# Token mixer of a vision tower: the kqv product contracted over 576 rows, with the last channel's weight row taken from all others and the last 64 rows worked in pairs

## The chip, the core and the metric

The kernel is one program on one core of a Trainium2 chip. The metric is the device time of one execution in microseconds (us), as the median of several runs. The engines are named as in the profile: PE is TensorE (matmuls and transposes), PEld its weight loads, DVE VectorE, ACT ScalarE, POOL GpSimd, SP SyncE, which issues transfers.

## The reference

The whole is a vision tower: a tokenizer with two "performer" blocks, two attentions, a mixture of experts, a state space layer and a gated mixture of experts. The change lies in the tokenizer's second performer block, here called the token mixer. What it computes, cut from the reference:

```python
def _ln(x, g, b):
    mu = jnp.mean(x, -1, keepdims=True)
    var = jnp.var(x, -1, keepdims=True)
    return (x - mu) * jax.lax.rsqrt(var + 1e-05) * g + b

def _performer(x, n1g, n1b, kqvw, kqvb, projw, projb, n2g, n2b, w1, b1, w2, b2, wrand):
    h = _ln(x, n1g, n1b)
    kqv = h @ kqvw + kqvb
    k, q, v = (kqv[..., :EMB], kqv[..., EMB:2 * EMB], kqv[..., 2 * EMB:])
    kp, qp = (_prm_exp(k, wrand), _prm_exp(q, wrand))
    ...
    y = v + (y @ projw + projb)
    h2 = _ln(y, n2g, n2b)
    return y + (jax.nn.gelu(h2 @ w1 + b1, approximate=False) @ w2 + b2)
```

In the token mixer x has 32 images of 256 tokens, each token 576 channels (9 taps of 64). `kqvw` is 576 x 192, all in fp32. A row of x less its mean sums to zero over the 576 channels.

## The kernel before, in words

`tokens` is the token mixer. It works in 16 steps of two images: 512 tokens as four tiles of 128 tokens. `X` holds the patches as they come, `hN` the normalised ones, `hT` the transposed ones, `W` the weights (256 columns: 192 of kqv and 64 of features made from them), `KQ` the product in PSUM, one tile in half a bank, tiles 0 and 1 in one bank and 2 and 3 in the next.

The contraction has 577 rows: 576 channels and a row of ones for the bias. `KT` cuts it into four chunks of 128 rows and one of 65. For each chunk k, `turn(i, k)` makes four transposes into a bank of PSUM, `keep(i, k)` copies the bank to `hT` on ScalarE, and `matmuls(i, j)` makes the five matmuls of tile j.

Each engine has its own program, written out in an order by hand and tied by semaphores. One loop over t lets several pairs of images be in flight. PE's step t is:

```
proj_matmuls(t-6), matmuls(t-1,0), keys_values(t-2), turn_queries(t-2), proj_turn(t-5), matmuls(t-1,1),
turn(t,0), turn(t,1), project_keys(t-2), turn_y(t-3), matmuls(t-1,2), turn(t,3), numerators(t-2),
mlp1(t-3), matmuls(t-1,3), mlp2(t-3), turn(t,4), turn(t,2)
```

The parts at t-5 and t-6 project finished tokens (`PX`, `PXT`, `PO`) and exist from steps 5 and 6 on. The waits that matter: `matmuls(i, 0)` waits for `z` of the pair before, since `KQ` has one buffer, and for all five `hT` chunks. `z` comes from `exponent` on DVE, behind `squares` and `values` on ACT, behind the last matmul of the pair (`kq`). `proj_turn(i)` waits for `po`, the copy of the projection's result by `proj_out` (L1128) on DVE, which stands in DVE's order behind `exponent` (L1067, L1071) and `normalise` (L1061). `normalise` waits for `rstd1` from `root` on POOL (L1008, L1010), which stands on POOL behind `bias_y` (L1028), which waits for `finish` on DVE (L1117), which waits for `mlp2` (L1342). SP issues per step 12 transfers for X (once `normalise` freed the buffer), 4 of results, 6 for `PX` and 1 of `PO`.

`Later` holds what the mixer needs ready: the stage ahead, `patches`, runs its parts beside its own work. `clear` (POOL, at that stage's step 4) zeroes tiles; `load` (SP) fetches weights once seven clears are done; `tensor` and `vector` fold gains and biases into `W` in three hops at the stage's end.

## Time and profile before

| what | value |
|---|---|
| median of 3 runs | 1924.81 us (1924.61 to 1925.4) |
| the profiled execution | 1919.23 us, its span 1917.5 us |
| PE busy in the span | 1602.2 us (84%) |
| DVE, ACT, POOL busy | 1080.6, 816.2, 736.7 us |
| kqv matmuls of the token mixer (L1279) | 640 records, 150.9 us |

The profile is of one execution, so a sum is made against its own 1919.23 us. One fp32 matmul is two records on PE and one transpose is one. PE's matmuls overlap at their ends, so what one costs is read from the start of one group to the start of the next and not from its busy time.

### The profile page before, as it was taken

Reading aid. Unit: us, or ns where it says so; the run is one execution under the profiler, and the core shown is the slowest. Engines: PE = TensorE matmul, PEld = TensorE weight load, DVE = VectorE, ACT = ScalarE, POOL = GpSimd, SP = SyncE. Lnnn points to the kernel's source line nnn. Section 1 sums busy time; section 2 is a strip of 40 time slices with the busy share of each in tenths; the row PEclk is TensorE's granted clock in tenths of the full one; section 3 lists DMA queues with packets and bytes.
Section 4 is the critical chain, followed back from the end, with each engine's and each line's share of the span. In section 5 each row is a group of like instructions: output and inputs, shape, how many; then the busy total and the mean of one; then the engine's idle time right before and its main releaser. Section 6 shows DMA issues by size and latency. Waiting matters only on the chain. (4 is left out here: it accounts for less than half of the span.)

```text
span 1917.5 us, 35003 instructions
## 1 busy us (share of the span) xinstructions
PE 1602.2 (84%) x11224; PEld 1231.6 (64%) x11225; DVE 1080.6 (56%) x3241; ACT 816.2 (43%) x1641; POOL 736.7 (38%) x680
## 2 busy tenths in 40 slices
PE   3889999968999976897988789996499477767997
PEld 2667777747888863775677779995377233347554
DVE  2678888856776633297267523331800599952332
ACT  0457777733555522283145533332355332324221
POOL 2557676721222204252423114442200399930232
PEclk9989999988999977897979669998599799967999
DMA  3243434323334222000000444442500666625321
GB/s 62 45 95 73 83 73 82 75 67 92 105 110 118 68 59 70 1 2 13 1 2 2 131 143 179 167 177 73 129 1 0 178 161 162 156 64 159 101 95 43
DMA packets 219149, 163.90 MB, mean 85 GB/s; under 512 B 115754, under 2 KB 198695, under 8 KB 218525
## 3 DMA queue, kind: packets, MB, share of 16 engines
q1 hardware_dynamic: 206135, 146.94, 28.8%
q0 software_dynamic: 6528, 14.19, 2.6%
q10 hardware_dynamic: 6374, 1.33, 0.4%
q8 instruction: 64, 1.05, 0.2%
q14 instruction: 48, 0.39, 0.1%
HBM read 106.05 MB, written 32.35 MB: 72 GB/s over the span
## 5 line engine op out<-in xcount | busy, mean ns | idle before, releaser
L2156 POOL TENSOR_TENSOR ssm_scan_prod<-ssm_scan_S,ssm_crep 128x1056 f32<-128x1056 f32 x48 | 159.4, 3320 | 146.8 <-DVE ssm_scan_S L2173 146.8
L1279 PE MATMUL a_psum<-a2w_W,a_hT 128*128 128x256 f32 (+1 forms) x640 | 150.9, 383 | 5.4 <-DVE a_z L1071 4.5
L755 PE MATMUL a_psum<-a_W,a_hT 126*128 126x256 f32 x512 | 135.3, 397 | 0.0
L1279 PEld LDWEIGHTS a_psum<-a2w_W,a_hT 128*128 128x128 f32 (+1 forms) x640 | 119.9, 192 | 21.2 <-issue 6.6
L2197 PE MATMUL ssm_scan_psum<-ssm_ST,ssm_EW 112*128 112x512 f32 (+1 forms) x288 | 106.0, 506 | 24.0 <-PEq L1908 20.4
L2173 DVE TENSOR_TENSOR_SCAN ssm_scan_S<-ssm_scan_X,ssm_scan_psum 128x1056 f32<-128x1056 f32 x48 | 113.0, 2354 | 5.5 <-ACT ssm_scan_psum L2185 1.2
L2813 ACT ACTIVATE moe_tiles_GT<-moe_tiles_psum,moe_tiles_mine 128x128 f32<-128x128 f32 x240 | 66.4, 376 | 110.6 <-PE moe_tiles_psum L2764 110.5
L2197 PEld LDWEIGHTS ssm_scan_psum<-ssm_ST,ssm_EW 112*128 112x128 f32 x288 | 52.3, 195 | 92.7 <-issue 69.7
L755 PEld LDWEIGHTS a_psum<-a_W,a_hT 126*128 126x128 f32 x512 | 91.1, 193 | 30.9 <-issue 21.9
L543 POOL TENSOR_TENSOR a_rstd<-a_rstd,a_mhalf 128x8 f32<-128x8 f32 x64 | 105.1, 1642 | 5.0
L2185 ACT ACTIVATE ssm_scan_psum<-ssm_scan_psum 128x1056 f32<-128x1056 f32 x48 | 49.7, 1035 | 121.3 <-PE ssm_scan_psum L2197 121.3
L2744 PE MATMUL moe_tiles_psum<-moe_W,moe_tiles_GT 128*128 x480 | 84.5, 326 | 0.0
L2865 DVE TENSOR_TENSOR moe_tiles_Y<-moe_tiles_psum,moe_B 128x192 f32<-128x192 f32 x40 | 14.3, 358 | 124.2 <-PE moe_tiles_psum L2744 124.2
L2053 PE MATMUL ssm_mlp_psum<-ssm_mlp_xT,ssm_mlp_W 96*128 96x260 f32 (+3 forms) x352 | 81.7, 392 | 2.6 <-SPq L1959 2.6
L1028 POOL TENSOR_TENSOR a_yb<-a_y,a2w_b 128x256 f32<-128x256 f32 x16 | 11.6, 725 | 177.1 <-DVE a_O L1117 165.3
L2709 POOL DMA_INDIRECT ys<-moe_tiles_Y,moe_target x40 | 39.4, 986 | 103.9 <-DVE moe_tiles_Y L2865 101.0
L563 POOL TENSOR_TENSOR a_yb<-a_y,a_b 128x512 f32<-128x512 f32 x32 | 40.8, 1277 | 96.9 <-DVE a_O L638 96.9
L2053 PEld LDWEIGHTS ssm_mlp_psum<-ssm_mlp_xT,ssm_mlp_W 96*128 96x128 f32 (+3 forms) x352 | 66.9, 190 | 16.4 <-issue 3.0
L2744 PEld LDWEIGHTS moe_tiles_psum<-moe_W,moe_tiles_GT 128*128 128x128 f32 x480 | 77.2, 190 | 0.0
L2699 POOL DMA_INDIRECT moe_tiles_X<-xs,moe_source x40 | 39.0, 975 | 81.3 <-POOLq L2307 69.4
L2210 PE MATMUL ssm_scan_psum<-ssm_scan_prod,ssm_SEL 128*32 128x264 f32 x384 | 32.8, 415 | 43.5 <-POOL ssm_scan_prod L2156 43.5
L2166 DVE TENSOR_TENSOR ssm_scan_X<-ssm_scan_grep,ssm_brep 128x1056 f32<-128x1056 f32 x48 | 59.2, 1233 | 17.0 <-DMA ssm_scan_grep<-gains 17.0
(654 smaller groups left out, 4059.0 us busy)
## 6 DMA issues: line engine op xcount, KB each, us to landing
ssm_scan_grep<-gains SPq DMA_DIRECT2D x48, 528.0 KB, 4.7
moe_tiles_mine<-moe_W SPq DMA_DIRECT2D x40, 579.0 KB, 3.1
a2w_X<-t SPq DMA_DIRECT2D x192, 96.0 KB
t<-a_O SPq DMA_DIRECT2D x128, 64.0 KB
xrows<-in_x SPq DMA_DIRECT2D x30, 192.0 KB
glu_tiles_mine<-glu_W1r SPq DMA_DIRECT2D x24, 234.5 KB, 3.2
a_X<-xrows SPq DMA_DIRECT2D x60, 91.9 KB, 3.0
a_PX<-t SPq DMA_DIRECT2D x96, 48.0 KB
```

Source lines behind the costliest of these rows:

```text
L543: nc.gpsimd.tensor_tensor(out[:], out[:], mhalf[:], ALU.pow).then_inc(s[done], 1)
L563: nc.gpsimd.tensor_tensor(yb[:], y[:], spread(b2[:], 1, tiles), ALU.add).then_inc(s["yb"], 1)
L755: last = nc.tensor.matmul(KQ[q][:, j, :], hT[0:MAIN, q, PARTS * j:PARTS * j + PARTS], W[0:MAIN, :], start=False, stop=True)
L1279: last = nc.tensor.matmul(KQ[:, j, :], hT[i % 2][0:rows, k, PARTS * j:PARTS * j + PARTS], W[0:rows, k, :], start=(k == 0), stop=(k == 4))
L2053: last = nc.tensor.matmul(ps[0:rows_, (n % 4) * BANK:(n % 4) * BANK + GROUP], W1[0:k, kb, c0:c0 + rows_], xT[0:k, kb, GROUP * g:GROUP * g ...
L2156: nc.gpsimd.tensor_tensor(prod[n % 2][:], S[n % 2][:], crep[:, cols], ALU.mult).then_inc(s_prod, 1)
L2166: nc.vector.tensor_tensor(X[n % 2][:], grep[n % NEWEST][:], brep[:, cols], ALU.mult).then_inc(s_x, 1)
L2173: nc.vector.tensor_tensor_scan(S[n % 2][:], X[n % 2][:], E[n % 2], 0.0, ALU.add, ALU.mult).then_inc(s_scan, 1)
L2185: nc.scalar.activation(E[n % 2], E[n % 2], ACT.Exp).then_inc(s_coef, 1)
L2197: last = nc.tensor.matmul(E[n % 2][:, a:b], EW[:, j, :], ST[:, j // (NCH // 2), HCOLS * h + a:HCOLS * h + b], start=True, stop=True)
L2744: last = nc.tensor.matmul(made(p), GT[p][0:w_, f, :], W2[0:w_, f, bass.ds(e, 1), :].rearrange("p a c -> p (a c)"), start=(f == 0), stop=(f ...
L2813: last = nc.scalar.activation(GT[1 - p][:, f, :], hidT(1 - p, f), ACT.Gelu, bias=mine[(n - 1) % RING][:, BIAS + f:BIAS + f + 1])
```

## The change

The contraction loses its 577th row. After the three hops of weight preparation a fourth makes two small matmuls with constant matrices (`lessall`, `lastmix`, made on POOL in `clear`): their sums take the weight row of channel 575 from every row of `W`. Since normalised channels sum to zero before gains, the product is the same, and row 575 is free: it takes the bias row, and in the data the last of the 64 remaining channels takes the ones. The last 64 rows of `W` then stand twice, in partitions 0 to 63 and 64 to 127.

`normalise` writes 512 channels to `hN` and 63 to a new tile `hR`, whose four slots hold tiles 0, 2, 1, 3, so that two tiles' 64 remaining channels lie side by side. Chunk 4 is two transposes of 128 columns (tiles 0 and 2, tiles 1 and 3) instead of four, its copy has 256 columns instead of 512, and its four matmuls have 64 rows each: tiles 0 and 1 from partitions 0 to 63, tiles 2 and 3 from 64 to 127. All four stand now ahead of the main ones in `matmuls(i, 0)`.

The diff, cut to its core:

```diff
         self.g2, self.n2b, self.b1r = (st.sbuf(n, [PARTS, 1]) for n in ("g2", "n2b", "b1r"))
+        self.lessall, self.lastmix = st.sbuf("lessall", [EMB + 1, PARTS]), st.sbuf("lastmix", [EMB + 1, 2, EMB])
         self.s_clear, self.s_w, self.s_raw, self.s_brow, self.s_gain, self.s_turn, self.s_wt, self.s_feat = (
...
         nc.gpsimd.memset(self.epst[:], EPS).then_inc(self.s_clear, 1)
+        nc.gpsimd.memset(self.lessall[:], 0.0).then_inc(self.s_clear, 1)
+        nc.gpsimd.memset(self.lastmix[:], 0.0).then_inc(self.s_clear, 1)
+        pool.wait_ge(self.s_clear, 9)
+        nc.gpsimd.affine_select(out=self.lessall[:], in_=self.lessall[:], compare_op=ALU.not_equal, fill=-1.0, base=1 - EMB,
+                                pattern=[[0, PARTS]], channel_multiplier=1).then_inc(self.s_clear, 1)
+        nc.gpsimd.affine_select(out=self.lastmix[:], in_=self.lastmix[:], compare_op=ALU.not_equal, fill=1.0, base=0,
+                                pattern=[[0, 2], [-1, EMB]], channel_multiplier=1).then_inc(self.s_clear, 1)
+        pool.wait_ge(self.s_clear, 11)
+        nc.gpsimd.affine_select(out=self.lastmix[:], in_=self.lastmix[:], compare_op=ALU.not_equal, fill=-1.0, base=1 - EMB,
+                                pattern=[[0, 2], [0, EMB]], channel_multiplier=1).then_inc(self.s_clear, 1)
+        pool.wait_ge(self.s_clear, 12)
+        nc.gpsimd.memset(self.lastmix[:, :, EMB - 1:EMB], 0.0).then_inc(self.s_clear, 1)
+        pool.wait_ge(self.s_clear, 13)
+        nc.gpsimd.affine_select(out=self.lastmix[:, :, EMB - 1:EMB], in_=self.lastmix[:, :, EMB - 1:EMB], compare_op=ALU.not_equal, fill=1.0,
+                                base=-EMB, pattern=[[0, 2], [0, 1]], channel_multiplier=1).then_inc(self.s_clear, 1)
...
             last.then_inc(self.s_turn, 1)
-        else:
+        elif hop == 2:
             pe.wait_ge(self.s_wt, 1)
             last.then_inc(self.s_feat, 1)
+        else:
+            pe.wait_ge(self.s_clear, 14)
+            pe.wait_ge(self.s_wt, 2)
+            nc.tensor.matmul(ps[:, two:two + 256], self.lessall[:], self.W[0:EMB + 1, 4, :], start=True, stop=True)
+            nc.tensor.matmul(ps[:, two + 256:two + 512], self.lastmix[:].rearrange("p a b -> p (a b)"), self.W[0:EMB + 1, 4, :], start=True, stop=True).then_inc(self.s_feat, 1)
...
             nc.vector.tensor_copy(self.WT[:, 4, 0:65], ps[:, two:two + 65]).then_inc(self.s_wt, 1)
-        else:
+        elif hop == 2:
             dve.wait_ge(self.s_feat, 1)
             nc.vector.tensor_copy(self.W[:, 0:4, 3 * EMB:], ps[:, three:three + 8 * FEATS].rearrange("p (k f) -> p k f", k=4))
-            nc.vector.tensor_copy(self.W[0:65, 4, 3 * EMB:], ps[0:65, three + 8 * FEATS:three + 10 * FEATS])
+            nc.vector.tensor_copy(self.W[0:65, 4, 3 * EMB:], ps[0:65, three + 8 * FEATS:three + 10 * FEATS]).then_inc(self.s_wt, 1)
+        else:
+            dve.wait_ge(self.s_feat, 2)
+            nc.vector.tensor_tensor(self.W[:, 0:4, :], self.W[:, 0:4, :], spread(ps[:, two:two + 256], 1, 4), ALU.add)
+            nc.vector.tensor_copy(self.W[:, 4, :], ps[:, two + 256:two + 512])
...
                     exponent(t - 2, 0)
-                if isinstance(t, int) and steps + 2 <= t < steps + 5:
+                if isinstance(t, int) and steps + 2 <= t < steps + 6:
                     later.vector(dve, ps, t - steps - 2)
...
                     sum_keys(t - 2)
-                if isinstance(t, int) and steps + 1 <= t < steps + 4:
+                if isinstance(t, int) and steps + 1 <= t < steps + 5:
                     if t == steps + 1:
...
     tiles, steps, width = 4, IMAGES // 2, 577
-    dim, COLS = 576, 256
+    dim, main, COLS = 576, 512, 256
     KT = later.KT
...
-        hN, hT = pair("hN", [PARTS, tiles, width]), pair("hT", [PARTS, 5, BANK])
+        hN, hR, hT = pair("hN", [PARTS, tiles, main]), pair("hR", [PARTS, tiles, EMB]), pair("hT", [PARTS, 5, BANK])
         stats = st.sbuf("stats", [PARTS, tiles, 2, 6])
...
             for p in range(2):
-                nc.gpsimd.memset(hN[p][:, :, dim:width], 1.0).then_inc(s["ones"], 1)
+                nc.gpsimd.memset(hR[p][:, :, EMB - 1:EMB], 1.0).then_inc(s["ones"], 1)
             nc.gpsimd.memset(v1[:, :, EMB:EMB + 1], 1.0).then_inc(s["ones"], 1)
...
                 for j in range(tiles):
-                    last = nc.vector.tensor_scalar(hN[i % 2][:, j, 0:dim], X[i % 2][:, j, :], mv[i % 2][:, j, 0:1], rstd[i % 2][:, j:j + 1],
-                                                   ALU.subtract, ALU.mult)
+                    nc.vector.tensor_scalar(hN[i % 2][:, j, :], X[i % 2][:, j, 0:main], mv[i % 2][:, j, 0:1], rstd[i % 2][:, j:j + 1],
+                                            ALU.subtract, ALU.mult)
+                for j in range(tiles):
+                    last = nc.vector.tensor_scalar(hR[i % 2][:, 2 * (j % 2) + j // 2, 0:EMB - 1], X[i % 2][:, j, main:dim - 1], mv[i % 2][:, j, 0:1],
+                                                   rstd[i % 2][:, j:j + 1], ALU.subtract, ALU.mult)
                 last.then_inc(s["norm"], 1)
...
                 wait(act, s["kq"], i - 1)
-                rows = KT[k][1]
-                nc.scalar.copy(hT[i % 2][0:rows, k, :], ps[0:rows, TB[k] * BANK:(TB[k] + 1) * BANK]).then_inc(s[f"th{k}"], 1)
+                n = BANK if k < 4 else half
+                nc.scalar.copy(hT[i % 2][:, k, 0:n], ps[:, TB[k] * BANK:TB[k] * BANK + n]).then_inc(s[f"th{k}"], 1)
...
                         pe.wait_ge(s["ones"], 5)
-                c0, rows = KT[k]
-                for j in range(tiles):
-                    last = nc.tensor.transpose(ps[0:rows, TB[k] * BANK + PARTS * j:TB[k] * BANK + PARTS * j + PARTS], hN[i % 2][:, j, c0:c0 + rows], ident[:])
+                for j in range(tiles if k < 4 else tiles // 2):
+                    frm = hN[i % 2][:, j, PARTS * k:PARTS * k + PARTS] if k < 4 else hR[i % 2][:, 2 * j:2 * j + 2, :].rearrange("p t c -> p (t c)")
+                    last = nc.tensor.transpose(ps[:, TB[k] * BANK + PARTS * j:TB[k] * BANK + PARTS * j + PARTS], frm, ident[:])
                 last.then_inc(s[f"t{k}"], 1)
...
                     wait(pe, s["z"], i)
-                for k, (_, rows) in enumerate(KT):
-                    last = nc.tensor.matmul(KQ[:, j, :], hT[i % 2][0:rows, k, PARTS * j:PARTS * j + PARTS], W[0:rows, k, :], start=(k == 0), stop=(k == 4))
+                    for h in range(2):
+                        for u in range(2):
+                            p0 = EMB * u
+                            nc.tensor.matmul(KQ[:, h + 2 * u, :], hT[i % 2][p0:p0 + EMB, 4, PARTS * h:PARTS * h + PARTS], W[p0:p0 + EMB, 4, :],
+                                             start=(h == 0), stop=False, skip_group_check=True)
+                for k in range(4):
+                    last = nc.tensor.matmul(KQ[:, j, :], hT[i % 2][:, k, PARTS * j:PARTS * j + PARTS], W[:, k, :], start=False, stop=(k == 3), skip_group_check=True)
                 if j == 3:
```

On PE, at the end of a full step of the mixer and the head of the next (`a_hN` and `a_hR` are normalised data, `a_hT` their transposes, `a2w_W` the weights). Before:

```order
L1279 MATMUL a_psum<-a2w_W,a_hT 128x256 x5
L1342 MATMUL a_psum<-a2w_w,a_G 128x128 [waits a2_gelu]
L1342 MATMUL a_psum<-a2w_w,a_G 128x128
L1270 MATMUL a_psum<-a2w_ident,a_hN 65x128 [waits a2_th1]
L1270 MATMUL a_psum<-a2w_ident,a_hN 65x128 x3
L1270 MATMUL a_psum<-a2w_ident,a_hN 128x128 [waits a2_gelu]
L1270 MATMUL a_psum<-a2w_ident,a_hN 128x128 x3
L1279 MATMUL a_psum<-a2w_W,a_hT 128x256 [waits a2_th3,a2_th4,a2_th2,a2_z,a2_th1,a2_th0]
L1279 MATMUL a_psum<-a2w_W,a_hT 128x256 x4
L1291 MATMUL a_psum<-a_kpq,a_v 65x32 [waits a2_exp,a2_ymul]
```

And with the change:

```order
L1312 MATMUL a_psum<-a2w_W,a_hT 128x256 x4
L1375 MATMUL a_psum<-a2w_w,a_G 128x128 [waits a2_gelu]
L1375 MATMUL a_psum<-a2w_w,a_G 128x128
L1298 MATMUL a_psum<-a2w_ident,a_hR 128x128 [waits a2_th1]
L1298 MATMUL a_psum<-a2w_ident,a_hR 128x128
L1298 MATMUL a_psum<-a2w_ident,a_hN 128x128 [waits a2_gelu]
L1298 MATMUL a_psum<-a2w_ident,a_hN 128x128 x3
L1309 MATMUL a_psum<-a2w_W,a_hT 128x256 [waits a2_th3,a2_th4,a2_th2,a2_z,a2_th1,a2_th0]
L1309 MATMUL a_psum<-a2w_W,a_hT 128x256 x3
L1312 MATMUL a_psum<-a2w_W,a_hT 128x256 x4
L1324 MATMUL a_psum<-a_kpq,a_v 65x32 [waits a2_exp,a2_ymul]
```

Two transposes are gone between `mlp2` and the next block; the first block has eight matmuls and the others four, where each had five.

On DVE, from `normalise` to `normalise_y` in a late step. Before:

```order
L1061 TENSOR_SCALAR a_hN<-a2w_X,a_mv,a_rstd 128x576 [waits a2_t2,a2_rstd1]
L1061 TENSOR_SCALAR a_hN<-a2w_X,a_mv,a_rstd 128x576 x3
L1128 COPY a_PO<-a_psum 128x192 [waits a2_h1,a2_pm]
L1110 TENSOR_SCALAR a_yn<-a_y,a_mv,a_rstd 128x64 [waits a2_yt,a2_rstd2]
L1110 TENSOR_SCALAR a_yn<-a_y,a_mv,a_rstd 128x64 x3
```

And with the change:

```order
L1086 TENSOR_SCALAR a_hN<-a2w_X,a_mv,a_rstd 128x512 [waits a2_t2,a2_rstd1]
L1086 TENSOR_SCALAR a_hN<-a2w_X,a_mv,a_rstd 128x512 x3
L1089 TENSOR_SCALAR a_hR<-a2w_X,a_mv,a_rstd 128x63 x4
L1156 COPY a_PO<-a_psum 128x192 [waits a2_h1,a2_pm]
L1138 TENSOR_SCALAR a_yn<-a_y,a_mv,a_rstd 128x64 [waits a2_yt,a2_rstd2]
L1138 TENSOR_SCALAR a_yn<-a_y,a_mv,a_rstd 128x64 x3
```

Four instructions more stand ahead of the copy to `PO`; nothing else on DVE moves there.

## Rows read from the trace of the kernel before

**Rows 1.** Stretches: us, busy us (records) by engine, then PEclk, DMA share, GB/s

```profile
428.90:441.45 12.55, 4.61 (x20) 3.88 (x21) 9.40 (x30) 2.93 (x5) 2.66 (x9) 0.50 0.28 67
591.66:607.31 15.65, 15.49 (x97) 14.02 (x97) 11.07 (x38) 8.23 (x16) 3.95 (x7) 1.00 0.45 130
```

**Rows 2.** PE in order of time: start, us, line, operation, shapes, count, idle before

```profile
498.00 2.40 PE L1279 MATMUL a_psum<-a2w_W,a_hT 128*128 128x256 f32 x10 [0.91 <-DVE a_z L1071]
...
588.71 0.61 PE L1342 MATMUL a_psum<-a2w_w,a_G 128*128 128x128 f32 x4
594.73 0.73 PE L1356 MATMUL a_psum<-a2w_ident,a_PX 128*128 128x128 f32 x5 [0.15 <-issue]
595.30 2.33 PE L1279 MATMUL a_psum<-a2w_W,a_hT 128*128 128x256 f32 x10
597.46 1.04 PE L1270 MATMUL a_psum<-a2w_ident,a_hN 128*128 128x128 f32 x8
598.34 0.33 PE L1307 MATMUL a_psum<-a2w_projw,a_kvT 65*128 65x65 f32 x2
...
604.37 0.61 PE L1342 MATMUL a_psum<-a2w_w,a_G 128*128 128x128 f32 x4
```

**Rows 3.** DVE in order of time, the mixer's start and one late step

```profile
433.90 2.05 DVE L1061 TENSOR_SCALAR a_hN<-a2w_X,a_mv,a_rstd 128x576 f32<-128x576 f32 x4 [1.41 <-POOL a_rstd L1010]
...
589.36 0.42 DVE L1117 TENSOR_TENSOR a_O<-a_psum,a_yb 128x256 f32<-128x256 f32 x1 [0.56 <-PE a_psum L1342]
...
591.94 2.42 DVE L1061 TENSOR_SCALAR a_hN<-a2w_X,a_mv,a_rstd 128x576 f32<-128x576 f32 x4 [0.98 <-POOL a_rstd L1010]
594.28 0.34 DVE L1128 COPY a_PO<-a_psum 128x192 f32<-128x192 f32 x1
594.55 0.97 DVE L1110 TENSOR_SCALAR a_yn<-a_y,a_mv,a_rstd 128x64 f32<-128x64 f32 x4
595.44 2.96 DVE L1046 BATCH_NORM_STATS2 a_stats<-a2w_X 128x6 f32<-128x288 f32 x8
```

**Rows 4.** POOL in order of time, the same late step

```profile
589.93 0.73 POOL L1028 TENSOR_TENSOR a_yb<-a_y,a2w_b 128x256 f32<-128x256 f32 x1 [11.54 <-DVE a_O L1117]
...
590.89 1.02 POOL L1010 TENSOR_TENSOR a_rstd<-a_rstd,a2w_mhalf 128x4 f32<-128x4 f32 x1
```

**Rows 5.** Who waited for whom in the mixer: total us, times, longest

```profile
PE a_psum L1279 <- DVE a_z L1071: 4.5, 4, 1.4
...
PE a_psum L1356 <- issue: 1.4, 9, 0.2
```

**Rows 6.** PE in order of time: narrow matmuls in two other stages

```profile
211.32 0.71 PE L749 MATMUL a_psum<-a_Wrem,a_RQ 32*128 32x256 f32 x8
211.97 1.13 PE L755 MATMUL a_psum<-a_W,a_hT 126*128 126x256 f32 x4
...
1300.93 0.94 PE L2761 MATMUL moe_tiles_psum<-moe_tiles_XT,moe_tiles_mine 64*128 64x128 f32 x12
1301.80 1.38 PE L2764 MATMUL moe_tiles_psum<-moe_tiles_XT,moe_tiles_mine 128*128 128x128 f32 x10
```

**Rows 7.** POOL and DVE in order of time, the stage ahead of the mixer

```profile
90.58 0.19 POOL L541 TENSOR_TENSOR a_rstd<-a_mv,a_eps 128x8 f32<-128x8 f32 x1
...
104.03 1.80 DVE L580 BATCH_NORM_STATS2 a_stats<-a_X 128x6 f32<-128x147 f32 x8 [9.62 <-DMA a_X<-xrows]
```

**Rows 8.** All engines in order of time, the end of that stage

```profile
422.52 2.02 PE L830 MATMUL a_psum<-a_w,a_G 128*128 128x128 f32 x8
...
424.58 0.69 DVE L638 TENSOR_TENSOR a_O<-a_psum,a_yb 128x512 f32<-128x512 f32 x1 [1.26 <-PE a_psum L830]
425.37 1.73 SPq L498 DMA_DIRECT2D t<-a_O  x4
...
428.95 2.97 DVE L1046 BATCH_NORM_STATS2 a_stats<-a2w_X 128x6 f32<-128x288 f32 x8 [3.67 <-PEq L202]
```

**Rows 9.** SP's queue in order of time, the same late step

```profile
594.39 7.62 SPq L99 DMA_DIRECT2D a2w_X<-t  x12
```

## The prediction, made before the change was run

> **What bounds the kernel now.** I read the stretches of the span first, then the token mixer's own stretch engine by engine in order of time, then who waits for whom there. All that the change touches lies in the token mixer, from 428.9 us on [rows 8], plus eight small instructions and one more hop of weight preparation in the stage ahead of it. In a full step of the mixer TensorE works 15.49 us of 15.65, at the full granted clock (1.00, 2.4 GHz), against 11.07 us of VectorE, 8.23 of ScalarE and 3.95 of GpSimd [rows 1]. TensorE is the bound, so what it is spared counts, as long as nothing else is late by then. Two things are nearly late. In four early steps TensorE waits for `z`, 4.5 us together [rows 5]: there a closed loop of TensorE, ScalarE and VectorE sets the step. In ten later steps there is a hole of 0.15 us ahead of line 1356 [rows 2], nine of them visible [rows 5]. That hole is the trace of a second loop: `mlp2` ends, VectorE's line 1117, GpSimd's 1028 and 1010, VectorE's 1061 and 1128, and only then may TensorE turn `PX` (its wait on `po`) [rows 3, 4]. Row by row: `mlp2` starts at 588.71 and line 1128 ends at about 594.6; line 1356 starts at 594.73 [rows 2, 3].
>
> **The change part by part: TensorE.** Five matmuls of 256 columns take from 595.30 to 597.46, 0.433 us each [rows 2]. The fifth of each tile, over 65 rows, costs as much as one over 128, so the four of them are 1.73 us a step. In their place stand four of 64 rows in two pairs. The nearest rows are the twelve records of line 2761, which are the same pattern (64 rows, halves of the array in turn, two banks): 1300.93 to 1301.80, 0.87 us for 12 records of 128 columns, and the eight records of line 749 (32 rows, 256 columns): 211.32 to 211.97, 0.65 us where one after the other they would need 1.73 [rows 6]. Line 749 is two passes of 0.213 us and 0.22 us over, which I read as the weights' load standing bare at the way in and at the way out; line 2761 fits this (six passes of 0.107 and 0.22). So four passes: 4 x 0.213 + 0.22 = 1.07 us. The gain is 0.66 us a step. Its bounds: 0.87 us (nothing bare) and 1.73 + 0.2 (pairs one after the other). In the steps that wait for `z` the load was bare already (2.40 against 2.33 us for the block [rows 2]), so there it is 0.73.
> Eight transposes take 597.46 to 598.34, 0.109 us each [rows 2]; two fewer a step are 0.22 us. They stand between `mlp2` and the next block, in the wait for `z`, so in the four steps that wait they bring nothing.
> All four narrow matmuls move into the first block of the step: that block grows from 2.16 to 2.80 us and the three others shrink by 0.43 each.
>
> **VectorE.** Normalising was four instructions of 576 elements, 591.94 to 594.28 = 2.34 us; undisturbed it is 2.05 [rows 3], so some 0.36 us of it is the last one being held while GpSimd's adds run. Now it is four of 512 and four of 63. Line 1110 is four of 64 elements: 594.55 to 595.44, 0.22 us each; four of 576 take 0.49 apart from the hold. Per element that is (0.49 - 0.22)/512 = 0.53 ns, so a 512 takes 0.46. Sum: 4 x 0.46 + 4 x 0.22 = 2.72 against 1.96, so the edit costs x = 0.76 us. Bounds: 0.3 (the small ones nearly hidden behind their neighbours) to 1.3 (their own 0.3 each and a second hold). I take 0.76, since line 1110 is the same operation on the same engine. The Trainium skill, "VectorE: DVE Perf Modes", section on the TRN2 errata, gives a VectorE instruction from SBUF to SBUF a fixed 58 cycles beside its elements; by that figure the four more would add about 0.24 us, an estimate, and the second loop would not bind. The rows of line 1110 speak against it; it is the second rival below.
>
> **The second loop after the change.** From line 1356 to `mlp2` it runs 594.73 to 604.37 = 9.64 us, all TensorE, with three blocks in it: 9.64 - 1.30 = 8.34. From `mlp2` to line 1356 it runs 588.71 to 594.73 = 6.02, all in the chain over VectorE and GpSimd: 6.02 + 0.76 = 6.78. Together 15.12 us, against 15.66 now (588.71 to 604.37 [rows 2]). TensorE's own work would be 15.49 - 0.66 - 0.22 = 14.6. So this loop binds, TensorE waits 0.4 to 0.5 us a step ahead of the `PX` transposes, and the step gains 0.54 instead of about 1.0. The cost that VectorE takes on is thus not hidden in these steps.
>
> **What has cover.** ScalarE's copy of chunk 4 has 256 columns instead of 512 and is not late now. SyncE issues 23 transfers a step at 0.635 us (twelve take 7.62 [rows 9]), 14.6 us, under 15.12; X has a whole step of slack. GpSimd's eight more instructions (about 1.9 us, from neighbours of 0.1 to 0.3 us and four waits) push `root` of the sixth image from 90.58 on, and TensorE's transposes behind it by 1.3 us, but VectorE stands still until an X transfer lands at 104.03 [rows 7], and SyncE waits only for the first seven clears, which stay where they were. The new hop: TensorE's last matmuls end near 424.5 [rows 8], at the half clock that the mixer's first stretch still has (0.50 [rows 1]); two matmuls of 256 columns there are 1.71 us, then on VectorE 1024 elements, twice line 638's 0.69 less its fixed part, 1.22, and a copy of 0.42, done near 428.1. What ends the block is the last stores, whose issue runs to 427.1 and whose data must land before the mixer starts at 428.9 [rows 8]. Covered by about 0.6 us; if that cover went, it costs that much and no more than 1.
>
> **The sum.** Start: first normalising +0.76, two transposes fewer at half clock (0.50 [rows 1]) -0.43: +0.33. Step 1 -0.66. Steps 2 to 4 -0.73 each, -2.2. Step 5 (`z` wait at its head, no `po` wait) -0.73 - 0.22 = -0.95. Steps 6 to 15: 10 x -0.54 = -5.4. Step 16 has no transposes and no normalising beside it: -0.66. Sum -9.5 us. The tail of dependent short work keeps its length. The profiled execution took 1919.23 us (span 1917.5), so it would be 1909.7; the median of the runs shown is 1924.81, 5.6 us above it, and I take the difference off that: 1915.3 us.
>
> **The rivals.**
> *Pairs don't overlap.* A block of four then costs 1.73 + 0.2 us. TensorE's work falls by nothing (-0.22 + 0.2) and it is the bound again: steps 6 to 15 gain only the 0.15 hole, the others lose 0.1 to 0.2: -0.4 us, 1924.4. The change would not do what it says. Lines 749 and 2761 speak against it, and both write different banks in turn, as the new ones do. The Trainium skill, "TensorEngine Tiling (Array Packing)", section on PSUM pressure, says that row tiles cannot use one PSUM bank at the same time; tiles 0 and 2, or 1 and 3, are in different banks here, so by that rule too they overlap. Chance 0.08.
> *The small instructions are cheap* (x at or under 0.3). Then TensorE's work is the bound, 14.6 us a step: -1.0 x 10 in place of -5.4, -14.1 us, 1910.7. Chance 0.10.
> *The hold spreads (slower).* VectorE's last line-1061 instruction now costs 0.36 us more when GpSimd works beside it. If four more of the eight were held so, x = 0.76 + 1.44 = 2.2, and ten steps change by -1.30 + 2.2 = +0.9: with the -4.1 of the other steps +4.9, 1929.7. It turns slower than before from x = 1.71. Against it: GpSimd runs only line 1023 (0.68 us) and short four-element work in that stretch, and one hold is all that it makes now. The Trainium skill, "SBUF - State Buffer", section on SBUF's two sides, calls the pair of ports that the two engines share an exclusive lock held for a whole instruction, which would fit more holds with more instructions. Chance 0.06.
> *Something with small slack is late* (`mlp2`'s VectorE step has 0.1 us left, the `PX` transfers of step 5 about 0.2, or the granted clock goes from 0.50 to 1.00 later at the mixer's start): 3 to 5 us of the gain go, 1919 or so. Chance 0.14.
>
> **How the numbers follow.** The forecast as worked out (x between 0.5 and 1.0, 1912 to 1918) has 0.62, and the time is 1915.3. The range 1910 to 1921.5 takes in it, the cheap case and the late case, and leaves out 0.14. A measurement of this kernel can tell about 0.2%, 3.8 us, from no change. Faster by more than that: the forecast, the cheap case and three quarters of the late one, 0.82. Within: overlap missing and the rest, 0.12. Slower: 0.06.
>
> **What the profile of the changed kernel would show.** The narrow matmuls in one block of 1.0 to 1.1 us to the next line; normalising at 3.1 us from its start to line 1128's; a wait of TensorE for `a_PO` of 0.4 to 0.5 us in ten steps; late steps of 15.1 us and early ones shorter by 0.73; waits for `z` longer by 0.2 each. The prediction is wrong if the late step is 14.7 (x is small), 15.5 (no overlap) or over 15.6 (holds), or if the mixer begins later than 428.9.

## The result, and the profile after

The changed kernel took 1921.17 us (median of 20 executions) against 1926.44 us for the kernel before in the same session: ratio 0.9972, 95% interval 0.9960 to 0.9984, so 0.28% less, 5.3 us. Two later repeats of the same kernel gave 0.9983 (0.9963 to 1.0002) and 0.9987 (0.9971 to 1.0003), which by themselves do not exclude that nothing changed. The forecast was 9.5 us, to 1915.3. The ratio applied to the 1924.81 us from which the forecast set out gives 1919.4, inside the range of 1910 to 1921.5. The direction was right, the size was not: little more than half of it came, and less in the two repeats.

The profiled executions alone would say that nothing changed: 1919.02 us after, 1919.23 us before. The mixer says otherwise. From its first VectorE instruction to the start of its last matmul it took 286.5 us before (428.95 to 715.43) and 280.7 us after (427.0 to 707.66), 5.8 us less (280.0 and 276.3 us in the two repeats). What follows it, untouched, took 1202.0 us before and 1209.6 after. Over all profiled kernels of this study that remainder lies between 1202 and 1217 us, whatever the mixer did, with some 310 to 342 us of it at the half clock (a granted clock of 0.50). So the mixer's own length is the finer measure here, and the whole time the judge.

Two stretches of the changed kernel (us, then busy us and records of PE, PEld, DVE, ACT and POOL, then PEclk, DMA share, GB/s): the mixer's start and one late step, as in [rows 1].

```profile
427.00:439.84 12.84, 4.19 (x18) 3.46 (x19) 9.74 (x33) 2.62 (x5) 2.63 (x9) 0.50 0.26 62
569.92:585.09 15.17, 14.93 (x95) 12.98 (x94) 11.79 (x42) 7.99 (x16) 3.92 (x7) 1.00 0.40 111
```

PE of the changed kernel in order of time (start, us, line, shapes, count, idle before). Line 1309 is the narrow block, 1312 the main matmuls, 1389 the `PX` transposes, 1375 `mlp2`, 1400 the projection:

```profile
497.94 0.73 PE L1389 MATMUL a_psum<-a2w_ident,a_PX 128*128 128x128 f32 x5 [0.62 <-DMA a_PX<-t]
...
585.09 1.14 PE L1309 MATMUL a_psum<-a2w_W,a_hT 64*128 64x256 f32 x8
586.16 1.99 PE L1312 MATMUL a_psum<-a2w_W,a_hT 128*128 128x256 f32 x8
587.99 0.61 PE L1324 MATMUL a_psum<-a_kpq,a_v 128*65 128x32 f32 x8
...
590.28 0.74 PE L1389 MATMUL a_psum<-a2w_ident,a_PX 128*128 128x128 f32 x5 [1.54 <-DMA a_PX<-t]
...
598.62 0.61 PE L1375 MATMUL a_psum<-a2w_w,a_G 128*128 128x128 f32 x4
...
599.74 1.89 PE L1400 MATMUL a_psum<-a2w_PW,a_PXT 128*128 128x192 f32 x10
601.56 1.13 PE L1309 MATMUL a_psum<-a2w_W,a_hT 64*128 64x256 f32 x8
...
604.90 0.31 PE L1332 MATMUL a_psum<-a2w_ident,a_kpq 128*128 128x128 f32 x1
605.46 0.74 PE L1389 MATMUL a_psum<-a2w_ident,a_PX 128*128 128x128 f32 x5 [0.25 <-issue]
```

The narrow block takes 1.07 us (585.09 to 586.16). From `mlp2` to the `PX` transposes it is 6.84 us (598.62 to 605.46), and back to `mlp2` 8.34 (590.28 to 598.62): a step of 15.18. Before it was 6.02 and 9.64. One late step is longer, 16.47 us, with 1.54 us of visible waiting for a transfer of `PX`, and the first `PX` waits 0.62.

VectorE of the changed kernel in the same late step, to hold against [rows 3]:

```profile
601.85 2.35 DVE L1086 TENSOR_SCALAR a_hN<-a2w_X,a_mv,a_rstd 128x512 f32<-128x512 f32 x4 [0.98 <-POOL a_rstd L1035]
604.13 0.97 DVE L1089 TENSOR_SCALAR a_hR<-a2w_X,a_mv,a_rstd 128x63 f32<-128x63 f32 x4
605.02 0.34 DVE L1156 COPY a_PO<-a_psum 128x192 f32<-128x192 f32 x1
```

Who waited for whom in the changed mixer (total us, times, longest), to hold against [rows 5]:

```profile
PE a_psum L1309 <- DVE a_z L1099: 5.4, 4, 1.6
...
PE a_psum L1389 <- DMA a_PX<-t: 3.0, 3, 1.5
...
PE a_psum L1389 <- DVE a_PO L1156: 1.5, 3, 0.7
```

And SyncE's queue there, to hold against [rows 9]; line 100 is X, 993 the result, 988 `PX`, 977 the stores:

```profile
558.30 8.07 SPq L100 DMA_DIRECT2D a2w_X<-t  x12
566.41 0.55 SPq L993 DMA_DIRECT2D h<-a_PO  x1
567.07 4.80 SPq L988 DMA_DIRECT2D a_PX<-t  x6
571.91 2.46 SPq L977 DMA_DIRECT2D t<-a_O  x4
574.42 7.61 SPq L100 DMA_DIRECT2D a2w_X<-t  x12
```

From 558.30 to 574.42 SyncE stands still for no more than some 0.1 us between groups (and once 0.25 us within the twelve) and needs 16.12 us for its 23 transfers, in a kernel whose step is 15.17. What it lost there makes its next round late, and with it the `PX` that TensorE waits 1.54 us for.

### The profile page after: what moved, and what is told of

It reads as the page before. It is cut to its first block and busy times, and to the rows that moved or that the text cites. A ratio compares the mean times of both kernels' runs of the same rounds, so it can differ in the third digit from the quotient of the medians.

```text
span 1917.3 us, 35025 instructions
## 1 busy us (share of the span) xinstructions
PE 1592.8 (83%) x11196; PEld 1214.8 (63%) x11197; DVE 1094.3 (57%) x3307; ACT 812.0 (42%) x1641; POOL 738.2 (39%) x687
## 5 line engine op out<-in xcount | busy, mean ns | idle before, releaser
L1312 PE MATMUL a_psum<-a2w_W,a_hT 128*128 128x256 f32 x512 | 123.4, 384 | 0.0
L1312 PEld LDWEIGHTS a_psum<-a2w_W,a_hT 128*128 128x128 f32 x512 | 94.1, 191 | 16.6 <-issue 5.6
```

Of the source, the lines that this page charges most:

```text
L1312: last = nc.tensor.matmul(KQ[:, j, :], hT[i % 2][:, k, PARTS * j:PARTS * j + PARTS], W[:, k, :], start=False, stop=(k == 3), skip_group_ch ...
```

## The experiments

The measure for all of them is the time of ten late steps, from the start of the first group of `PX` transposes to that of the eleventh: 156.54 us before, 153.05 after. In the diffs, names are those of the kernel. e5, e6 and e11 ran once each (1931.59, 1917.79 and 1937.63 us), so only their traces count; every reading of steps is of one profiled execution.

**The changed kernel again (e1, e14).** No edit.

> The changed kernel once more, unchanged, as the mark for the next three on the same chip. Sum theory (my forecast): the mixer is 9.5 us shorter than before, ratio 0.995. Lost-in-transfers theory (from the trace after: three waits of TensorE for PX transfers, 3.0 us, late steps 15.17 instead of 15.12, early steps -0.65 instead of -0.73): the mixer is 5.8 us shorter, ratio 0.997. From its start (427.0 in the trace after) to the last projection's start the mixer takes 280.7 us; before it took 286.5.

> The changed kernel unchanged, as the mark for e12 and e13 on their chip and to narrow the change's own figure: by the 20 runs of the result ratio 0.9972, by e1 0.9983; the trace's 5.8 us in the mixer say 0.997. By the forecast's 9.5 us, 0.995.

Ten steps of 152.74 and 152.31 us, times of 1922.52 and 1922.29 us, ratios 0.9983 and 0.9987. The steps that no transfer holds are 15.17 to 15.19 in both. `PX` was late in both: over the whole mixer TensorE waits 3.1 us for it in e1 and 4.8 in e14 (3.2 of these behind the ten late steps). The long late step is the sixth again, 16.15 us in e1 and 15.53 in e14, after one of 15.32. The sum theory's 0.995 lies outside all three intervals.

**VectorE's order (e2), SyncE's order (e3), both (e4).**

```diff
-                if live(t - 1):
-                    normalise(t - 1)
                 if live(t - 7):
                     proj_out(t - 7)
+                if live(t - 1):
+                    normalise(t - 1)
...
                 if live(t):
-                    load(t)
-                if live(t - 8):
-                    put(t - 8)
+                    load(t, range(4))
                 if live(t - 6):
                     reload(t - 6)
+                if live(t):
+                    load(t, range(4, IN_DMAS))
+                if live(t - 8):
+                    put(t - 8)
```

> The changed kernel with VectorE's copy of the projection's result (proj_out) ahead of normalise instead of behind it. Loop theory: the 6.84 us from mlp2 to the PX transposes fall to TensorE's own 6.6 us, late steps go from 15.17 to 14.92 us, and nothing waits for a_PO: 10 x 0.25 = 2.5 us less than e1. SyncE theory: SyncE's 23 transfers a step already take 15.2 to 16.1 us, so the wait for a_PO only turns into a wait for the a_PX transfers, the late steps stay at 15.1 or more on average, and the gain is 0 to 1 us.

> The changed kernel with SyncE's order turned: four X transfers, then the six for PX, then the other eight for X, then the result; before, PX stood behind all twelve. Same number of transfers. SyncE-order theory: PX lands 5 us earlier, TensorE's 3.0 us of waits for a_PX go, step 5 and the one long late step (16.47) come back to 14.9 to 15.2: 2.5 to 3.0 us less than e1. If instead the transfers themselves are slow (memory, not order), the waits stay and the time is that of e1. If SyncE as a whole binds, X is late instead and VectorE's statistics wait for it: time as e1 or above.

> Both of the moves of e2 and e3. If the loop and the order on SyncE are the two limits, late steps are TensorE's own 14.9 us throughout, step 5 too: 5 to 5.5 us less than e1, ratio 0.994 to 0.995. If SyncE's total is a third limit (23 transfers at 0.635 us are 14.6, stretched 15.2 or more), late steps stay near 15.2 and the gain is that of e3 alone, about 3 us.

e2: five steps fall to 14.74 to 14.88 us, the others take 15.06 to 15.82; ten take 150.71. Nothing in the late steps waits for `a_PO`. Among the waits of TensorE from step 5 on stands now

```profile
PE a_psum L1389 <- DMA a_PX<-t: 2.7, 5, 0.9
```

so both theories hold a part: the loop was the limit, and SyncE is the next one. Its time is 1916.09 us, ratio 0.9958 (0.9932 to 0.9984), the lowest of all. e3: all ten steps are 15.15 to 15.19, 151.81 together; the late `PX` is gone, the loop remains; its time is 1919.13 us, ratio 0.9977 (0.9956 to 0.9999). In e3 and in e4 step 5 takes 14.74 us, against 15.54 in the changed kernel: the late transfers of `PX` had cost it 0.80 us. e4: eight of ten steps are 14.74, one 16.51 and one 15.29, together 149.72, its time 1918.95 us, ratio 0.9968 (0.9947 to 0.9989). A step of 14.74 is less than the 14.9 that I expected as TensorE's own; the section on the prediction says why. The two bad ones stand elsewhere: not `PX` but X was late. VectorE's waits in e4's late steps:

```profile
DVE a_stats L1073 <- DMA a2w_X<-t: 8.3, 7, 3.0
```

This row is of a kernel in which the six transfers of `PX` stand in the middle of X's twelve. In the changed kernel itself X is never late in these steps: by the semaphores in the trace all twelve have landed 3.0 to 5.8 us before VectorE reads them, in e4 1.0 us before at most and often only as VectorE waits. So the slack that the prediction called a whole step was 3 to 6 us, and e4's order spends it.

**The disputed cost, doubled (e5).**

```diff
+                for j in range(tiles):
+                    nc.vector.tensor_scalar(hS[i % 2][:, j, 0:EMB - 1], X[i % 2][:, j, main:dim - 1], mv[i % 2][:, j, 0:1],
+                                            rstd[i % 2][:, j:j + 1], ALU.subtract, ALU.mult)
```

> The changed kernel with four more VectorE instructions of 63 elements in normalise, written to a spare tile: the disputed cost x doubled from 0.83 to about 1.7 us. Loop theory (mlp2, finish, the additions, root, normalise, proj_out, PX): late steps go from 15.17 to 16.0 to 16.1 us, all of it in the wait ahead of the PX transposes, and SyncE's 15.2 to 15.6 us fit under it, so no wait for a_PX is left in the late steps. If SyncE's queue set the late steps, they would stay near 15.2. If VectorE and GpSimd hold each other more with more instructions, the step is over 16.2.

Every late step is 16.06 or 16.07 us, 0.89 longer, which is what the four instructions take on VectorE:

```profile
605.12 2.35 DVE L1086 TENSOR_SCALAR a_hN<-a2w_X,a_mv,a_rstd 128x512 f32<-128x512 f32 x4 [0.98 <-POOL a_rstd L1035]
607.39 0.97 DVE L1089 TENSOR_SCALAR a_hS<-a2w_X,a_mv,a_rstd 128x63 f32<-128x63 f32 x4
608.29 0.96 DVE L1092 TENSOR_SCALAR a_hR<-a2w_X,a_mv,a_rstd 128x63 f32<-128x63 f32 x4
609.17 0.34 DVE L1159 COPY a_PO<-a_psum 128x192 f32<-128x192 f32 x1
```

608.29 - 607.39 and 609.17 - 608.29 are 0.90 and 0.88. The loop theory is borne out to a hundredth. The hold by GpSimd does not grow with the number of instructions, which was the rival of the spreading hold. And with 16 us a step SyncE keeps up: no wait for `PX` in a late step.

**Do the pairs overlap (e6, e11)?** e6 changes the order of the four narrow matmuls, e11 takes all of them from the upper half (on top of e9, below):

```diff
-                    for h in range(2):
-                        for u in range(2):
+                    for u in range(2):
+                        for h in range(2):
                             p0 = EMB * u
```

```diff
-                            p0 = EMB * u
+                            p0 = 0
```

> The changed kernel with the four narrow matmuls in another order: the two of the array's upper half after one another, then the two of the lower half, so that only the middle two can overlap. Pairs-overlap theory: 3 of 4 passes instead of 2, each of two records of 0.213: the block takes 1.5 us instead of 1.07, TensorE's own step goes from 14.74 (e4) to 15.2, and late steps stay at the loop's 15.17 or rise to 15.2. If the records queue by halves and all four run one after another, 1.9 us, and late steps of 15.6. If the pairs did not overlap in the first place, 1.07 stays.

> e9 with all four narrow matmuls taking their 64 rows from the upper half of the array, twice the same rows, so that nothing can overlap (tiles 2 and 3 get the wrong data for their last 64 channels). Pairs-overlap theory: the block takes 4 x 0.433 = 1.73 us or a little more, not 1.07, and TensorE's own step goes from 14.74 to 15.3 to 15.6. If a matmul of 64 rows were cheap by itself, the block stays at 1.07 and the step at 14.74.

PE in e6, then in e11:

```profile
586.69 1.14 PE L1309 MATMUL a_psum<-a2w_W,a_hT 64*128 64x256 f32 x8
587.76 1.99 PE L1312 MATMUL a_psum<-a2w_W,a_hT 128*128 128x256 f32 x8
```

```profile
565.08 1.99 PE L1309 MATMUL a_psum<-a2w_W,a_hT 64*128 64x256 f32 x8
567.00 1.99 PE L1312 MATMUL a_psum<-a2w_W,a_hT 128*128 128x256 f32 x8
```

e11 (tiles 2 and 3 get the wrong data for their last 64 channels): 1.92 us, and all late steps 15.59: without overlap the block costs 0.85 more, so the pairs do overlap. e6 by itself could not tell: the block stays at 1.07 us. My reckoning of 1.5 was wrong, since it took it that the lower half's matmuls wait behind both of the upper half. They don't: in e6 the records of the two halves start 0.013 to 0.014 us apart, in the changed kernel 0.006 to 0.007. Its ten steps are 153.15, as after, again with one late `PX` (a step of 16.36).

**The kernel before, with e4's two moves (e7).**

> The kernel before with the two moves of e4 (proj_out ahead of normalise, PX ahead of eight of the X transfers). Theory that both limits came with the change: before, the loop stood only 0.16 us over TensorE's 15.49, and no PX transfer was late in a full step, so late steps go from 15.65 to 15.5 and the whole gains 1.5 us, ratio 0.999. If the moves are good whatever TensorE does, the gain is that of e4 against e1, 4 to 5 us, ratio 0.9975.

All ten steps are 15.31 us, 153.13 together, 3.4 us less than before and not 1.5; the ratio is 0.9980 (0.9959 to 1.0000). So in these ten steps the two moves alone bring the kernel before as much as the change does (153.05). TensorE needs 15.31 us and not the 15.49 that it is busy [rows 1]. PE in e7, and then in e16 (below), which shows the changed kernel with nothing in TensorE's way:

```profile
599.80 0.61 PE L1344 MATMUL a_psum<-a2w_w,a_G 128*128 128x128 f32 x4
600.25 1.04 PE L1272 MATMUL a_psum<-a2w_ident,a_hN 128*65 128x128 f32 x8
601.12 1.79 PE L1369 MATMUL a_psum<-a2w_PW,a_PXT 128*128 128x192 f32 x10
602.75 2.32 PE L1281 MATMUL a_psum<-a2w_W,a_hT 128*128 128x256 f32 x10
604.91 0.61 PE L1293 MATMUL a_psum<-a_kpq,a_v 128*65 128x32 f32 x8
605.36 0.31 PE L1301 MATMUL a_psum<-a2w_ident,a_kpq 128*128 128x128 f32 x1
605.50 0.71 PE L1358 MATMUL a_psum<-a2w_ident,a_PX 128*128 128x128 f32 x5
```

```profile
555.97 1.13 PE L1310 MATMUL a_psum<-a2w_W,a_hT 64*128 64x256 f32 x8
557.04 1.99 PE L1313 MATMUL a_psum<-a2w_W,a_hT 128*128 128x256 f32 x8
558.87 0.61 PE L1325 MATMUL a_psum<-a_kpq,a_v 128*65 128x32 f32 x8
...
568.21 0.38 PE L1299 MATMUL a_psum<-a2w_ident,a_hR 128*128 128x128 f32 x2
568.43 0.60 PE L1299 MATMUL a_psum<-a2w_ident,a_hN 128*128 128x128 f32 x4
568.89 1.89 PE L1401 MATMUL a_psum<-a2w_PW,a_PXT 128*128 128x192 f32 x10
570.71 1.14 PE L1310 MATMUL a_psum<-a2w_W,a_hT 64*128 64x256 f32 x8
```

Projection and first block were 1.63 + 2.16 = 3.79 us and are now 1.82 + 1.07 + 1.83 = 4.72: 0.93 more. By my terms it should have been 1.07 - 0.43 = 0.64. The group of ten ahead of the narrow block costs 0.19 more than before, and the main block behind it 0.10 more than its four times 0.433: there is a cost at the way in and one at the way out that the 1.07 did not hold. They are not the price of overlapping: in e11, where all four stand on one half, the group ahead takes the same 1.82 us and the one behind the same 1.83. Nor of the order of the two halves (e6: 1.82 and 1.83). Three blocks shrink by 1.30 and the transposes by 0.19 (0.87 to 0.68). TensorE's own step falls by 0.57, from 15.31 to 14.74, not by 0.88.

**Ways to free SyncE (e8, e9, e10, e12, e13).** e8 is e4 with three X transfers issued by ScalarE, e9 is e2 with the stores on ScalarE, e12 the same with the stores at the end of its step; e10 and e13 are the kernel before with the moves of e9 and e12.

ScalarE in e8, in e9 and in e12:

```diff
                     keep(t, 2)
+                    if live(t + 2):
+                        act.wait_ge(s["norm"], t + 1)
+                        later.load_x(act, t + 2, range(IN_DMAS - 3, IN_DMAS))
```

```diff
+                if live(t - 3):
+                    store(t - 3)
                 if live(t - 1):
                     exponential(t - 1)
```

```diff
                     proj_keep(t - 4)
+                if live(t - 3):
+                    store(t - 3)
```

> e4 with three of the twelve X transfers of a step issued by ScalarE, behind its copies of the transposes and ahead of exponential. SyncE-total theory: in e4 SyncE issues for 14.9 to 15.7 us a step against TensorE's 14.74, and that is where its two late steps (16.51 and 15.29) come from; with 20 instead of 23 transfers (13.3 us) all late steps are 14.74 and the time is 2 to 2.5 us under e4, ratio 0.9945 to 0.996. If the late step came from a transfer that was slow to land, it stays. If ScalarE cannot bear 1.9 us more, keys_values waits for exp and steps rise above 14.74.

> The changed kernel with proj_out ahead of normalise (as e2) and the four stores of a step issued by ScalarE ahead of exponential instead of by SyncE ahead of the X transfers. Theory from e4 and e8: X has no whole step of slack; its transfers start when normalise frees the buffer, take 7.6 us to issue and some 5 us to land, and whatever stands ahead of them or between them on SyncE (stores, PX) makes VectorE's statistics late. With the stores gone SyncE issues 19 transfers, 12.1 us, X first: no wait for X or PX in the late steps, all ten at TensorE's own 14.74, the time 5 to 6 us under e1, ratio 0.9945 to 0.9955. If ScalarE's 2.5 us for the stores push exp too late, keys_values waits for exp and steps exceed 14.74. If memory is what makes X late, steps over 15 remain.

> The kernel before with the same two moves as e9. From e7: TensorE's own step there is 15.31 us, and the ten late steps fall from 15.65 to it: 3.4 us less than before, ratio 0.998. The change measured with both limits away is then e9 against e10: 10 x 0.57 in the late steps and 0.65 in each of the others, 8 to 9 us in the mixer. If the moves bring before as much as after, e9 and e10 differ by no more than the 5 to 6 us that the kernels differ by now.

> e9 with the four stores at the end of ScalarE's step, behind proj_keep, where ScalarE stands idle for 2.24 us, instead of ahead of exponential, where they pushed exp late. Theory: e9 showed X and its statistics in time with 19 transfers on SyncE and lost only by keys_values waiting for exp (4.8 us) and by PX; now exp is in time, the stores overrun the hole by 0.3 to 0.7 us, which gelu's 0.4 us of slack takes up nearly. Late steps at TensorE's own 14.74 to 14.9, the mixer 4 to 5 us shorter than e1's, time 4 to 5 us under e14. If what remains late is PX (5.3 us in e9, its six transfers now behind all twelve for X) steps of 15.2 to 16.4 remain and the time is that of e14.

> The kernel before with the same moves as e12, so that the change can be measured with neither its VectorE cost nor SyncE's queue in the way. TensorE's own step before is 15.31 (e7): ten late steps at 15.31 to 15.4. The change is then e12 against e13: 10 x 0.57 in the late steps and about 0.65 in the first five and the last, 8 to 9 us less first transposes' 0.3: this would say that the forecast's 9.5 was the price of the matmuls, and that the rest was lost to what surrounds them. If e12 and e13 differ by 6 us only, the lost part is not in the loop nor in the transfers.

All five missed. e8: ten steps 150.35, no better than e4, time 1919.88 us, ratio 0.9974 (0.9955 to 0.9993); X is still late, and more often. VectorE's and SyncE's waits in its late steps:

```profile
DVE a_stats L1073 <- DMA a2w_X<-t: 13.0, 9, 2.1
```

```profile
SPq L988 <- DMA t<-a_O: 11.4, 10, 3.1
```

SyncE has three transfers less, but it stands 11.4 us waiting for stores to land before it may go on to `PX` and then to the rest of X, and ScalarE's three go out last, in one late round done at 540.10 us, 2.2 us after SyncE's nine. Which of the two makes X late, e8 does not separate. In e9 (ten steps 153.98, time 1928.34, ratio 1.0027, 1.0006 to 1.0048) X goes first again, as in the changed kernel, and no VectorE wait for X is left. But `PX` is late (3.3 us in e9 and in e12), and the stores hold ScalarE's `exp` back, in e12 (156.86, ratio 1.0076, 1.0052 to 1.0100) its copy of the queries. TensorE's waits from step 4 on in e9 and in e12:

```profile
PE a_psum L1389 <- DMA a_PX<-t: 3.3, 4, 1.4
PE a_psum L1324 <- ACT a_kpq L1215: 2.3, 6, 1.0
```

```profile
PE a_psum L1357 <- ACT a_Q L1225: 3.8, 10, 0.7
```

In e12 I had looked at the 2.24 us of idle time ahead of `yT` and overlooked that `keep_q` runs between. e10 loses at `exp` (9.8 us of TensorE's waits; 162.33, ratio 1.0064, 1.0042 to 1.0087), e13 at `PX` (2.3) and the queries (0.9; 158.18, ratio 1.0054, 1.0036 to 1.0072). Each of the four has stops of its own, so they say nothing on the change.

**One transfer a step to GpSimd (e15, e16, e17).** e15 is e4, e16 is e2 and e17 is e7, each with `put` on GpSimd between its two additions.

```diff
                 if live(t - 2):
                     bias_v(t - 2)
+                if live(t - 6):
+                    put(t - 6)
+                if live(t - 2):
                     bias_y(t - 2)
```

> e4 (proj_out ahead of normalise, PX ahead of eight of the X transfers) with the transfer of each result (put, one a step) issued by GpSimd between its two additions instead of by SyncE. SyncE-total theory: SyncE's 23 transfers take 14.9 to 15.7 us a step in e4 against TensorE's 14.74; with 22, 14.3 to 15.1, nearly all late steps are 14.74, the ten together 147.4 to 148.5 against 149.72 in e4 and 152.3 to 153.0 in the changed kernel: 4 to 5 us under e1 and e14, ratio 0.996. If GpSimd's issue (up to 1 us) delays its second addition, mlp2's result is finished late, and z, and steps rise over 15.

> e2 (proj_out ahead of normalise, order on SyncE as in the changed kernel: stores, all twelve X, then PX) with put on GpSimd. If only the number of transfers on SyncE matters, the 3.4 us of PX waits in e2's late steps go as in e15 and both give the same. If the order matters too, PX stays late in some steps: ten late steps of 149 to 151 against e15's 147.4 to 148.5.

> The kernel before with all three moves of e15. Its ten late steps stand at TensorE's own 15.31 already in e7, so putting one transfer elsewhere brings nothing: 153.1 for the ten, time as e7, ratio 0.998. The change with its two surroundings freed is e15 against e17: ten late steps shorter by 0.57 each, 5.7 us, and the mixer by 6.5 to 8.5 us in all, ratio e15 to e17 of 0.996. By the forecast's prices it would be 0.88 each.

e16, of which I had expected less, is clean: nine of ten steps 14.74 to 14.77 and one 14.87, 147.58 together. TensorE's only wait ahead of line 1390 in those steps is

```profile
PE a_psum L1390 <- DMA a_PX<-t: 0.8, 1, 0.8
```

which belongs to the first of them. e15 missed its 147.4 to 148.5: it has eight steps at 14.74 to 14.79, one of 15.23 and one of 19.45, together 152.64, with VectorE waiting for X:

```profile
DVE a_stats L1074 <- DMA a2w_X<-t: 9.2, 7, 4.2
```

In the long step the last X was issued by 559.1 us and VectorE could begin only at 564.6, so that transfer was also slow to land; TensorE stood idle 2.8 us by 568.0, and its granted clock was 0.50 from 569.2 to 572.6. The order counts: with `PX` amid the twelve (e3, e4, e8, e15) X is late in three to nine steps, with X first (e16) in none. That the number counts as well is the likely reading of e16 against e2 (one transfer less, 147.58 against 150.71), on one trace each. e17 is 153.13, the same as e7 to a hundredth. e16 against e17 is the change with its surroundings freed: 5.55 us in ten steps, the 0.57 a step read off the rows above, less what one step of 14.87 took back. The mixer is 276.1 us in e16 and 283.1 in e17, 7.0 us less, where 6.5 to 8.5 were expected. Times: e15 1918.91 us (ratio 0.9959, 0.9938 to 0.9980), e16 1916.41 us (0.9963, 0.9942 to 0.9983), e17 1920.33 us (0.9980, 0.9965 to 0.9995). e2 and e16 are the fastest versions of this study; their intervals overlap that of the changed kernel, but ten late steps take 150.71 and 147.58 us in them against 152.31 to 153.05 in its three traces.

## Why the prediction was right or wrong

The forecast, term by term, against the profiled executions. A step runs from the start of its first block to that of the next.

| part | forecast us | measured us |
|---|---|---|
| start, to the first block | +0.33 | +0.34 |
| step 1 | -0.66 | -0.78 |
| steps 2 to 4 | -2.2 | -1.93 |
| step 5 | -0.95 | +0.16 |
| steps 6 to 15 | -5.4 | -3.52 |
| step 16 | -0.66 | -0.56 |
| tail | 0 | +0.47 |
| sum | -9.5 | -5.8 |

Of the missing 3.7 us, 2.1 are late transfers of `PX` (1.30 in one late step, 0.80 in step 5), 0.7 the edges of the narrow block, 0.6 the second loop and 0.5 the tail; step 1 gave 0.1 back (each rounded). Two steps of the prediction failed: that SyncE's 23 transfers are covered, and that the gain on TensorE is 0.66 us a step.

**The narrow block: its own size right, its surroundings missed.** 1.07 us was forecast and measured. The term that failed is the gain of 0.66 us a step. With the cost at the way in (0.19) and at the way out (0.10) it is 0.37. In the late steps the second loop hid this, a cover for 0.3 us that the forecast had not counted on: luck. In steps 2 to 4 and 16 the way out shows, some 0.1 each (the way in lies in the wait for `z`), and in step 5 both, 0.3. The way out could be read before the run, next to line 749 of [rows 6]. Line 755, four records of 256 columns, in the kernel before, once behind a group of full height and once behind the narrow one, both at the clock of 1.00:

```profile
202.97 1.03 PE L755 MATMUL a_psum<-a_W,a_hT 126*128 126x256 f32 x4
```

```profile
211.97 1.13 PE L755 MATMUL a_psum<-a_W,a_hT 126*128 126x256 f32 x4
```

The Trainium skill, "TensorEngine Tiling (Array Packing)", section on tiling modes, says that changing the mode, not merely the tile, drains TensorE. That is a rule against this change that I had not weighed, and the rows of e16 fit it, at 0.3 us a step for going in and coming out; they show the cost, not what TensorE does in that time.

**The small instructions: right.** x was 0.76 forecast and 0.83 measured (605.02 - 601.85 = 3.17 against 2.34). At the undisturbed start, the four of 512 and four of 63 took from 431.96 to 434.68, the 2.72 us of the sum. The 0.07 more is the hold beside GpSimd's addition, 0.44 instead of 0.37 us. e5 puts the small ones at 0.22 us each. The same section of the Trainium skill from which I took 58 cycles ("VectorE: DVE Perf Modes", on the TRN2 errata) adds that this figure under-predicts and that the measured fixed term is about 150 cycles. The rows of the undisturbed start give 0.458 us for 512 elements and 0.222 for 63, so 0.53 ns an element and 0.19 us fixed. By the section's 0.96 GHz that is some 180 cycles, an estimate: nearer to 150 than to 58. The trace does not agree with the first figure, and the rival that I drew from it had little behind it.

**The second loop: right, to 0.06 us.** 8.34 was forecast and measured for the way over TensorE, 6.78 against 6.84 for the way over VectorE, 15.12 against 15.17 to 15.18 a step. Ten steps: 0.6 us of the missing gain. The wait for `po` was forecast at 0.4 to 0.5 us; the hole that shows is 0.24 to 0.25, but from line 1332 to line 1389 it is 0.56 us (604.90 to 605.46), against 0.15 in e16, and the step is 0.43 over TensorE's own 14.74. So the wait was of the forecast size. e2 and e5 are the evidence that this loop set the step.

**SyncE: wrong, and the largest single miss.** The prediction put its 23 transfers at 14.6 us, "under 15.12; X has a whole step of slack". The cover failed, and X's slack was 3.0 to 5.8 us and not a step, though in this kernel X never came late. 0.635 us a transfer is the row of an undisturbed dozen; [rows 9] showed that one dozen and I took it for all. In the changed kernel SyncE needed 16.12 us for one round. A round of 15.17 us, over the 15.12 already, stood in the trace of the kernel before:

```profile
547.42 8.26 SPq L99 DMA_DIRECT2D a2w_X<-t  x12
...
560.11 2.48 SPq L952 DMA_DIRECT2D t<-a_O  x4
```

One late step of 16.47 us (+1.30) and 0.80 of step 5's 1.11 (its other 0.3 are the narrow block's edges) are 2.1 us of the missing 3.7; e3 took both away by its order on SyncE alone. I had named step 5's transfers, with 0.2 us of slack, as a rival ("something with small slack is late", 1919 us, chance 0.14). That case came, in step 5 and in a late step that I had not named. That its 1919 meets the measured time is in part luck, since the transfers are little more than half of what was lost.

**The wait of 0.15 us before: misread.** The hole ahead of line 1356 [rows 2] stands for 0.34 us: e7 took the wait away and the step went from 15.65 to 15.31. In e7 line 1356's group begins at 605.50, before line 1299's record ends (605.36 + 0.31), so a hole counted from that record's end is too small. From line 1299 to line 1356 it was 0.47 us before and is 0.14 in e7 (605.36 to 605.50). The row of the kernel before:

```profile
594.26 0.31 PE L1299 MATMUL a_psum<-a2w_ident,a_kpq 128*128 128x128 f32 x1
```

For the sum this did not matter, since it was made from starts and not from busy times. For TensorE's own step it did: 15.49 - 0.88 = 14.6 should have been 15.31 - 0.57 = 14.74.

**The rest.** The new hop was hidden: it ended on VectorE near 425.3 us, the mixer began at 427.0. The waits for `z` grew by 0.22 us each, as forecast. Step 1 lies partly at the half clock and took 13.50 us here, 13.58 and 13.53 in the repeats and 11.79 in e6, so its 0.12 us is within what it moves by itself. The 0.47 us of the tail lie in short dependent work at the half clock (0.50); it fell to that 10 us after the last large block both before and after. Where it stayed at 1.00 for 20 to 26 us behind that block, in e14 and e2, the tails took 31.5 us, against 34.7 before, 35.1 after and 34.2 in e1, so this term moves without any edit of the tail. What made the tail differ by 0.47 us between before and after is not shown.

What stays open: why single transfers take up to 1.57 us to issue where most take 0.57 to 0.63. The runs show when SyncE falls behind, not what stretches an issue. The stretched ones fall in much the same stretches of all traces: 1.24 us near 551 us in the kernel before, 1.16 near 553 and 1.57 near 569 in the changed one.

## What to carry to other kernels

Spare the bounding engine, and the next limit is the one whose slack you have read off a single row: for a queue take a whole round at its worst, not one group at its best. A wait in TensorE's timeline can be larger than the hole that shows (0.34 us for 0.15 here, 0.43 for 0.25), so measure it from start to start against a step that does not wait. And a narrow form of matmul costs at its edges: compare the groups before and behind it as well as the block itself.

## What the runs showed of the hardware

- Matmuls on the two halves of the array run side by side in either order: four of 64 rows and 256 columns take 1.07 us in whichever of the two orders they are written (e6), and 1.92 us when all are on one half (e11).
- A group of 64 rows between groups of full height costs 0.19 us at its way in and 0.10 us at its way out, at the clock of 1.00 (e7 and e16), also when all of it stands on one half (e11).
- VectorE's instructions of 63 elements cost 0.22 us each, and the hold on normalising beside GpSimd's work does not grow with their number (0.90 and 0.88 us for two groups of four, e5).
- The stages behind the mixer, the same code in all runs, took 1202 to 1217 us in the profiled executions: one execution of this kernel cannot show a gain of 5 us, though its mixer can.
